# A whitening, normalising and windowed-attention kernel: statistics and the first unit moved between mixing steps, PE waits moved inside groups

## The reference

```
x = x + zca(groupnorm32(x)) * weight + bias        # zca: 16 groups of 4 channels, proj = cov^(-1/2)
x = x + window_attention(batchnorm(groupnorm32(x)))
# zca: cov = mean of xg xg^T over all images and pixels + 1e-4 I ; proj = V diag(e^-1/2) V^T
# attention: windows of 7x7 tokens, 16 heads of 16 (q, k: 128 outputs of 64 channels), softmax,
#            v = relu(tok @ v_w^T), out = softmax(q k^T * scale) v
```

## Time and profile before

| | |
|---|---|
| median of 3 runs | 506.59 us (506.07 to 508.24) |
| profiled execution | 506.08 us |
| its span | 504.4 us |
| mean granted PE clock | 0.962 |
| PE busy | 449.0 us, 89% of the span, 17474 instructions |
| DVE / ACT / POOL busy | 336.2 / 294.7 / 190.7 us |

### The profile page before, as it was taken

The page is one execution under the profiler, slowest core; times in us unless marked ns, Lnnn a source line. Parts: engine busy times, 40 slices in busy tenths (PEclk is TensorE's granted clock), DMA queues, the critical chain, the costliest instruction groups (busy, mean ns, idle before and its releaser), DMA issues. The chain is left out here.

```text
span 504.4 us, 38739 instructions
## 1 busy us (share of the span) xinstructions
PE 449.0 (89%) x17474; PEld 361.0 (72%) x17474; DVE 336.2 (67%) x1077; ACT 294.7 (58%) x515; POOL 190.7 (38%) x158
## 2 busy tenths in 40 slices
PE   8999814985878999999999999999999999999964
PEld 8898713321666788888887887888788788878853
DVE  1544478883356777777777777777777777777744
ACT  2322210564656677767767776777677677767731
POOL 4071000002124455445544554454455445544512
PEclk9999956999699999999999999999999999999988
DMA  8970000001111414243241424324142433414232
GB/s 300 418 315 3 3 0 1 1 0 40 60 70 66 128 66 143 81 127 121 94 136 64 135 87 130 109 99 143 64 129 87 136 96 104 145 71 127 80 85 66
DMA packets 31567, 52.08 MB, mean 103 GB/s; under 512 B 6176, under 2 KB 21024, under 8 KB 30624
## 3 DMA queue, kind: packets, MB, share of 16 engines
q1 hardware_dynamic: 31520, 51.50, 30.3%
HBM read 12.95 MB, written 12.85 MB: 51 GB/s over the span
## 5 line engine op out<-in xcount | busy, mean ns | idle before, releaser
L309 POOL TENSOR_TENSOR X<-X,otok 128x392 f32<-128x392 f32 x63 | 107.3, 1703 | 193.0 <-DVE otok L713 193.0
L680 DVE TENSOR_REDUCE rmax<-ps 113x16 bf16<-113x784 f32 x128 | 120.8, 944 | 36.3 <-PE ps L866 36.2
L891 PE MATMUL ps<-diag,qk_all 64*49 64x98 f32 x4096 | 130.1, 246 | 0.2 <-ACT prob_all L360 0.2
L360 ACT ACTIVATE prob_all<-ps 113x784 f32<-113x784 f32 x128 | 105.7, 826 | 36.0 <-PE ps L898 34.7
L891 PEld LDWEIGHTS ps<-diag,qk_all 64*49 64x49 f32 x4096 | 110.6, 122 | 21.3 <-issue 15.2
L898 PE MATMUL ps<-mdiag,sel 64*49 64x98 bf16 x2048 | 112.2, 203 | 0.2 <-DVE mdiag L688 0.2
L303 POOL TENSOR_SCALAR xs<-X,affined 128x392 f32<-128x392 f32 x64 | 69.4, 1085 | 90.8 <-DVE affined L671 77.0
L375 ACT ACTIVATE vst<-ps 49x256 f32<-49x256 f32 x256 | 97.0, 379 | 11.4 <-PE ps L851 8.0
L367 ACT ACTIVATE qk_all<-ps 128x784 f32<-128x784 f32 x64 | 52.8, 825 | 71.9 <-PE ps L835 71.9
L697 DVE RECIPROCAL rden<-ps 128x98 f32<-128x98 f32 x64 | 49.4, 771 | 37.2 <-PE ps L914 37.2
L898 PEld LDWEIGHTS ps<-mdiag,sel 64*49 64x49 bf16 x2048 | 66.6, 101 | 0.5 <-issue 0.4
(11 more groups left out here) (161 smaller groups left out, 363.6 us busy)
## 6 DMA issues: line engine op xcount, KB each, us to landing
diag<-qk_all SPq DMA_DIRECT2D x256, 98.0 KB, 2.0
out<-X SPq DMA_DIRECT2D x30, 392.0 KB, 4.7
X<-x_in SPq DMA_DIRECT2D x7, 1024.0 KB, 16.1
X<-x_in SPq DMA_DIRECT2D x7, 544.0 KB, 16.9
X<-x_in SPq DMA_DIRECT2D x4, 256.0 KB, 3.7
out<-X SPq DMA_DIRECT2D x2, 294.0 KB, 3.8
X<-x_in SPq DMA_DIRECT2D x2, 192.0 KB, 4.6
out<-X SPq DMA_DIRECT2D x2, 98.0 KB, 2.4
```

The lines of the kernel that those rows point to most:

```text
L309: g.tensor_tensor(rows_of(u), rows_of(u), otok[u % 2][:].rearrange("p k a s -> p k s a"), ALU.add).then_inc(S["x_ready"], 1)
L360: a.activation(prob[u % 3][0:ROW, k].rearrange("p h g x j q -> p h (g x j q)"), ps[0:ROW, B_ST:B_ST + 2, 0:8 * POS], ACT.Exp, scale=SCALE) ...
L680: v.tensor_reduce(rmax[u % 3][0:ROW, :, 8 * k:8 * k + 8], ps[0:ROW, B_S:B_S + 2, 0:8 * POS].rearrange("p h (v q) -> p h v q", q=POS), AX.X ...
L891: mm(ps[64 * e:64 * e + POS, B_ST + hh, col:col + 2 * POS], qk[u % 3][r, g, k, 2 + x_, :], diag[u % 3][r, e::2, g, k, x_, :], start=True, ...
```

## The change

1. The warm-up at the start has 8 matmuls in place of 20, and ACT runs one small Copy before the first chunk.
2. BN's reciprocal root (`rsqrt(bninv...)`) and its product stand in stage 2, behind the three `vec_ready` instructions and ahead of the wait for `vec4_ps`, and not between mixing steps 19 and 21. The variance plus epsilon is written during the Gram stage.
3. Newton-Schulz: T comes from the sum itself. A fifth column of `zy`, written during the Gram stage, holds the eye term, and the sum over five elements gives T. The separate instruction goes. The scalings are folded into constants (`grown`).
4. Mixing: the second statistics stand as a block between steps 0 and 8 (`AT_SUMS`, `AT_AFFINE` = 3, 10, before 11 and 26). In steps 3 and 7 ACT takes both halves. The banks are 4,5 and 6,7 in turn, and 2,3 in place of 6,7 in the last four steps.
5. The work of iterations -2 and -1 stands between mixing steps: `project_qk(0)` ahead of step 15, `project_qk(1)` ahead of 18, the first scores and v of unit 0 ahead of 24, the second scores ahead of 27, `turn_max(0)` ahead of 30, with the ACT and DVE parts at the same steps. ACT zeroes the banks `B_ST` behind step 28 instead of in stage 2.
6. PE's register waits: `need("xs_ready")` and `need("v_ready")` of the next `project_qk` stand ahead of `weigh_values`; `need("max0")` stands ahead of the last quarter of `sum_weights`.

```diff
+AT_SUMS, AT_AFFINE = 3, 10
+AT_QK, AT_S, AT_MT = (15, 18), (24, 27), 30
...
-        B_MIX = (2, 4)
+        B_MIX = [4 if n % 2 == 0 else 6 if n < MIX - 4 else 2 for n in range(MIX)]
...
+        act_both = {3, 7}
...
+            a.activation(rden[:], ident[:, 0:2 * POS], ACT.Copy)
...
+            for n in range(MIX):
...
+                if n == AT_QK[0]:
+                    keep_qk(0)
+                if n == AT_QK[1]:
+                    keep_qk(1)
+                if n == AT_S[0]:
+                    keep_v(0)
+                mix(n)
+                if n == MIX - 4:
...
+                    a.activation(ps[:, B_ST:B_ST + 2, :], diag[0][:].rearrange("p j g k a s -> p (j g k a s)")[:, 0:1024].rearrange(
+                        "p (b c) -> p b c", b=2), ACT.Copy).then_inc(S["psum_zero"], 1)
-            for i in range(-2, UNITS + 1):
+            for i in range(0, UNITS + 1):
...
+            dve.wait_ge(S["std2_ready"], 1)
+            rsqrt(bninv[:, 2:3], bninv[:, 0:1], bninv[:, 1:2], t8b[:, 0:1])
+            chain(v.tensor_tensor(bninv[:, 2:3], bninv[:, 2:3], prm[:, 2:3], ALU.mult))
             dve.wait_ge(S["vec4_ps"], 1)
...
-                    chain(v.tensor_tensor(prods[:, 0], rows(Z), cols(Y), ALU.mult))
-                    chain(v.tensor_reduce(ms[:], prods[:, 0], AX.X, ALU.add))
-                t_step = v.scalar_tensor_tensor(ms[:], ms[:] if n > 0 else Y, -s * s / 3 * grown * grown, eye4[:],
-                                                ALU.mult, ALU.add)
+                    chain(v.tensor_tensor(zy[:, n, :, :, 0:ZG], rows(Z), cols(Y), ALU.mult))
+                    t_step = v.tensor_reduce(T, zy[:, n], AX.X, ALU.add)
...
-            warm_up(20)
+            warm_up(8)
...
-            def project_qk(u, at):
+            def tokens_there(u, at):
 
                 need("xs_ready", at)
                 need("v_ready", at)
+
+            def project_qk(u):
...
                 for c in range(4):
                     k, hh = divmod(c, 2)
+                    if c == 3 and first:
+                        need("max0", at)
...
                     scores_for_exp(u, 1, at)
+                if has(i + 3):
+                    tokens_there(i + 3, later)
                 if has(z):
                     weigh_values(z, at)
...
-                    rest(1 + r, pe.snap(3 * q + 4 + r), pe.snap(64 * q + 64 * ((2 + r) // 3 + 1)))
-                    project_qk(4 + r, pe.snap(3 * q + 5 + r))
+                    rest(1 + r, pe.snap(3 * q + 4 + r), pe.snap(3 * q + 5 + r), pe.snap(64 * q + 64 * ((2 + r) // 3 + 1)))
+                    project_qk(4 + r)
```

More of the change, by code:

```diff
@@ L212, in give, with mixed @@
                 eng.sem_inc(S[n], CREDIT[n])
+        act_both = {3, 7}
+        by_dve = [n for n in range(MIX) if n not in act_both]
+        def mixed(eng, n, m):
+            if m == 0 or n in act_both:
+                after(eng, "mix_act", n + 1)
+            else:
+                after(eng, "mix_dve", by_dve.index(n) + 1)
         def place(u):
@@ L341, in mix @@
                 act.wait_ge(S["mix_ps"], n + 1)
[L342 to L354, removed]
+                for m in range(2 if n in act_both else 1):
+                    ins = a.activation(X[:, p, :].rearrange("p (a i w) -> p i a w", a=WS, i=NW)[:, QI * m + ii],
+                                       ps[:, B_MIX[n] + m, 0:392].rearrange("p (a w) -> p a w", a=WS), ACT.Identity,
+                                       bias=dvecd[:, m, p:p + 1])
+                ins.then_inc(S["mix_act"], 1)
             def weights(u, k):
@@ L610, in _ @@
             dve.wait_ge(S["dd_ready"], 1)
-            mix(0)
             dve.wait_ge(S["ag_ps"], 1)
@@ L717, in _ @@
             dve.wait_ge(S["zeros_ready"], 3)
-            for i in range(-1, UNITS + 1):
+            for n in range(13, MIX):
+                if n in AT_S:
+                    maximum(0, AT_S.index(n))
+                if n == AT_MT:
+                    spread_max(0)
+                mix(n)
+            for i in range(0, UNITS + 1):
                 s, z = i + 1, i - 1
@@ new lines, in _ @@
+            for n in range(MIX):
+                if n == AT_SUMS:
+                    small("sums2_ready", 1, ps[:, 0, 0:2 * PAIRS], pairm[:], sd[:].rearrange("p a n -> p (a n)"), "gmean2_ps")
+                if n == AT_AFFINE:
+                    pe.wait_ge(S["affine_ready"], 2)
+                    for m in range(2):
+                        ins = mm(ps[:, 1, 64 + 2 * PAIRS * m:64 + 2 * PAIRS * (m + 1)], dupm[:, m].rearrange("p g c -> p (g c)"),
+                                 affine[:].rearrange("p k n -> p (k n)"), start=True, stop=True)
+                    ins.then_inc(S["affine_ps"], 1)
+                if n == AT_QK[0]:
+                    pe.wait_ge(S["const_dma"], 48)
+                    pe.wait_ge(S["zeros_ready"], 3)
+                    tokens_there(0, 1)
+                    project_qk(0)
+                if n == AT_QK[1]:
+                    tokens_there(1, 2)
+                    project_qk(1)
+                if n == AT_S[0]:
+                    scores_for_max(0, 0, 2, 64)
+                    project_v(0, 2)
+                if n == AT_S[1]:
+                    need("max0", 2)
+                    scores_for_max(0, 1, 2, 64)
+                if n == AT_MT:
+                    turn_max(0, 2)
+                mix(n)
@@ L947, in rest @@
                 if has(z):
-                    sum_weights(z, at)
+                    sum_weights(z, at, has(s))
                 if has(s):
+                    if not has(z):
+                        need("max0", at)
                     scores_for_max(s, 1, at, landed)
```

175 lines of the change are left out of this document (84 added, 91 removed).

## The result

The changed kernel takes 509.02 us, median of 20 runs (507.22 to 512.53), where the kernel before takes 506.64 (20 runs, 504.37 to 509.34): a ratio of 1.0051, interval 1.0032 to 1.0069. That is 2.4 us slower; the forecast was 505.1, which is 1.0 us faster than the profiled execution that its sum started from (506.1) and 1.5 under the median of before, and it gave "slower" a chance of 0.19.

The account below looks back on a forecast made before the run. PE bounds the Gram stage, a DVE chain the statistics; the changed loop is bound by a circle through PE, DVE and POOL. Sum: 506.1 - 9.6 before the steady loop + 8.6 in it = 505.1 us; forecast's range 499.5 to 509.5, overall 487 to 510.

Parts of the forecast that it names:

- The loop: 57 steady iterations: period rises from 5.55 to 5.70 us because weigh_values now waits for xs, +8.6 us in all.
- the circle: Steady loop: weigh_values, DVE, POOL's add and normalise, back to weigh_values; taken as 5.50 us, a floor for the iteration.
- the way: Steady loop: from POOL's end to PE's next weight load, taken as 0.20 us, bounds 0.05 and 0.35.
- slower than before: Rival for the loop: both waits passed only after POOL ends, period 5.80, 510.8 us; decides above 5.72; chance 0.10.
- What PE gains at `project_qk` is lost in the wait: Steady loop: freeing the gap ahead of project_qk, at most 0.23 us, brings nothing because PE waits for POOL instead.
- `max0` hidden behind the wait: Steady loop: the max0 wait inside sum_weights is hidden behind PE's wait for POOL; no cost added.
- Hidden waits: Rival for the loop: PE's queue covers the waits, each iteration loses 0.20 us, -11.4, 485.1 us; chance 0.20.
- The start: Shorter warm-up ahead of the Gram stage: transposes begin sooner but run into the loads; -1.6 us, bounds 0 and -3.7.
- Statistics: BN chain +0.3 us, nine Newton-Schulz steps without one instruction -1.7; together -1.4, bounds -1.9 to -0.8.
- Mixing: 32 mixing steps plus four added prices: iteration 0's project_qk(2) starts at 124.0 in place of 129.85, -5.8 us.
- Iteration 0: First loop iteration: PE at full clock, ACT ends it; 5.8 us in place of 6.65, -0.8 us.
- Iterations 1 to 3: Loop iterations ahead of the steady ones: same code fetches, keep their 22.4 us.

Follow-up runs that it names:

- e2: The kernel before with only both waits of the next project_qk moved ahead of weigh_values in the loop: 520.2 us, ratio 1.030 to before, period 5.78.
- e12: The changed kernel with only POOL's order altered, a unit's tokens normalised one add earlier: 486.3 us, ratio 0.959 to before, period 5.43.
- e9: The changed kernel with only the v_ready wait back ahead of project_qk: 500.2 us, ratio 0.986 to before, period 5.66.
- e11: The changed kernel with only the max0 wait back ahead of the second scores_for_max: 509.1 us, ratio 1.004 to before, period 5.78.
- e5: e4 with the max0 wait also back ahead of the second scores_for_max: 484.4 us, ratio 0.956 to before, period 5.37.
- e4: The changed kernel with only the xs_ready wait back ahead of project_qk: 487.9 us, ratio 0.966 to before, period 5.43.
- e1: The changed kernel with both the xs_ready and v_ready waits back ahead of project_qk: 498.8 us, ratio 0.988 to before, period 5.62.
- e10: e5 with more warm-up matmuls before mixing, 18 for 14 and 6 between the small matmuls: 485.3 us, ratio 0.956 to before, period 5.36.
- e6: e4 with the xs_ready wait ahead of project_qk made twice in a row: 494.7 us, ratio 0.976 to before, period 5.51.
- e3: The changed kernel with both waits between weigh_values and turn_max: 505.4 us, ratio 1.000 to before, period 5.74.
- e7: The kernel before, old front kept, with the waits of e5 in its loop: 496.7 us, ratio 0.980 to before, period 5.37.

## Why the prediction was wrong

The mechanism was right and two of its sizes were not; the sum of a loss and a gain of nearly the same size fell on the other side.

- **The loop, +8.6 us forecast, +13.1 measured.** This is the step that failed. I took the circle as 5.50 and the way as 0.20, 5.70 in all. Measured over 56 iterations are 5.53 and 0.22, and 0.03 more from the weight load to the first matmul, which stood in no term of mine although the circle was counted from matmul to matmul: 5.78. The circle itself is no longer than it was: in the trace of before its mean over the loop is 5.52 already (without the first round, where PE stops for 1.34), and I took a rounder value below it. I had written that each 0.05 us is 2.9 us of the total: 0.08 is 4.6, more than four times my forecast gain of 1.0. It came out as the rival "slower than before" had it, with its mechanism, its place and a period (5.78) between its turning point (5.72) and its price (5.80). To give that side 0.10 while my own value lay 0.02 from the turning point was too little. The range that I gave the forecast had a slip too: with 0.05 in the period and 1.5 in the front it begins at 500.7, not 499.5.
- **"What PE gains at `project_qk` is lost in the wait"**: shown, by e2 and e12. The gap ahead of `project_qk` is gone in the changed kernel and its period is longer all the same.
- **The way, half of it for the second wait**: right in kind and nearly in size (0.12 and 0.11; I had 0.10 and 0.1), by e9.
- **`max0` hidden behind the wait**: shown by e11; without the circle it costs 0.06 (e5), which I had not priced.
- **Hidden waits, 485.1 us, chance 0.20**: not what happened. In the changed kernel PE waits for POOL in all 56 iterations looked at. The Trainium skill, "TensorE: Matmul & The Clock Gate", in the section "Architectural detail: the array is 16× 32×32, not 1× 128×128", gives PE's queue 64 instructions. No run here shows that depth; what they show is that the work ahead of the wait did not cover it: PE stood idle for POOL 16.0 us in all. The time that the rival named is still what the loop gives once the circle is cut: 484.4 to 487.9 in e4, e5 and e12.
- **The start, -1.6**: right in size, 1.5 by the first small matmul behind the stage, and for the reason given, the load at 11.1. That it came out is in part luck: PE was ahead of that load by 0.26 us, not by the 2.1 that the prediction's rate gave it, and a start slower by more than that would have eaten into the gain.
- **Statistics, -1.4**: the step is 1.37 (forecast 1.38). Start and statistics together should bring the first mixing step 3.0 sooner; it is 2.56 sooner in the profile with the lower clock, and 3.1 in e1 (86.25), where the clock held.
- **Mixing, -5.8**: undersized. From the first mixing step to `project_qk(2)` are 40.49 us before and 33.24 or 33.25 in each of the seven profiles of the new front in which the clock held: -7.2. Which of the four prices in that sum was too high is not shown. `project_qk(2)` starts there at 119.40 (e12) to 119.97 (e4), not at about 121 (e10, with its longer warm-up, at 120.91). In the changed kernel's own profile it is 122.14, with 1.5 us lost in the first three steps (4.13 from the first to what follows the third, against 2.62 in e1).
- **Iteration 0, 5.8 forecast**: 5.91. **Iterations 1 to 3, unchanged**: 23.06 against 22.36. PE's stops for nothing that the profile shows add up to 5.5 us in them; they were 4.8 before and are 3.3 to 6.1 in the other profiles (4.2 in e11, where the three iterations take 22.3). That these stops are code fetched the first time, as I took them, no run tests.

So the profile that was read for the result had the clock and the stops against it: -7.75 at iteration 4, where the six others with the same front and the full clock have -10.7 (e11) to -12.0 (e1) and the forecast had -9.6. With these in front, +13.1 in the loop and +0.3 behind it the sum is +1.4 to +2.7; the medians differ by 2.4. The gain in front was larger than forecast, and the loop ate all of it.

## What to carry to other kernels

Before a wait is moved forward past other work of its engine, write down what its releaser itself waits for, all the way round: where that leads back to the group that the wait now stands in front of, the sum of the durations round the circle is a floor for the period. If this sum is within a per cent or two of today's period, no chance should rest on the sign; measure the circle over many iterations, take the mean as it is, and leave out no step on the way from the releaser's end back to the instruction that the circle was counted from. Two waits moved together can be of opposite worth (here `v_ready` free, `xs_ready` 20 us), so move them one at a time; and the cheapest cure may be on the other engine, as POOL's order was here.

## What was not expected

- A register-valued wait that is satisfied costs PE nothing ahead of `project_qk` when it stands alone, 0.08 us as the second in a row, and 0.19 with the register's arithmetic there too (e4, e6, e1). The gap of 0.23 in the earlier trace rows was so not the price of waiting, but of what stands in a row.
- The same two waits and arithmetic cost nothing ahead of `weigh_values` (e12, period 5.43 as e4), and 0.31 ahead of `turn_max` with its own wait (e3).
- The fall of the granted clock to half between warm-up and mixing happens in some executions and not in others of nearly the same order, with the old front (e7) as with the new. PE's two idle stretches alone don't decide it: they are 0.59 and 0.88 us in the changed kernel, where the clock fell, and 0.79 and 0.88 in e1, where it held.
